# Twelve maxima of the second softmax phase moved into the product stage, tail maxima in pairs, the first tile's scores and exponentials spread over the phase steps

## The reference

```
query = hidden_states @ Wq ; keyt = enc @ Wk ; valt = enc @ Wv
hs      = _mha(query, keyt, valt)                       # 2048 rows against 150 keys
ca_q1   = einsum('btc,th->bch', ca, Wq_ca)[:, indices]  # indices: 384 rows spread over 2048
ca_hs1  = _mha(ca_q1, residual, residual)               # 384 distinct queries against 2048 rows of x
ca_hs2  = _mha(ca_hs1 @ Wq, ca @ Wk_ca, ca @ Wv_ca)     # against 4 tokens
out     = (hs + ca_hs2) @ Wout + b_out + residual
```

## Time and profile before

| | |
|---|---|
| Median of 3 runs | 1694.64 us (1678.9 to 1694.96) |
| The profiled execution's own time | 1688.81 us |
| Its span | 1687.0 us |
| Granted TensorE clock, mean | 0.957 |
| PE busy | 1591.4 us, 94% |
| DVE busy | 811.0 us, 48% |
| ACT busy | 623.1 us, 37% |
| Chain that ended last | PE 86%, DVE 6%, ACT 4% |

### The profile page before, as it was taken

One profiled execution on the slowest core, in us unless ns is written; L12 is line 12 of the kernel. 1 busy time (PEld: TensorE's weight loads), 2 busy tenths in 40 slices (PEclk: granted clock), 3 DMA queues, 4 the chain that ended last, 5 costly groups with the idle time before them and its releaser, 6 DMA issues.

```text
span 1687.0 us, 24707 instructions
## 1 busy us (share of the span) xinstructions
PE 1591.4 (94%) x10327; PEld 1283.8 (76%) x10327; DVE 811.0 (48%) x1624; ACT 623.1 (37%) x1309; POOL 2.8 (0%) x12
## 2 busy tenths in 40 slices
PE   6699989999999989999999998999999999899999
PEld 5584379899986338999988435999898733898998
DVE  4457453453446724435335654354444672534533
ACT  0144742233242662323324275233233357322422
POOL 0000000000000000000000000000000000000000
PEclk9798999999999889999999799999999978999999
DMA  3461001130153000213025200112103500011101
GB/s 128 159 203 58 1 18 48 52 143 16 40 183 117 32 1 18 90 49 112 24 94 175 86 1 7 51 60 84 67 32 142 173 32 1 18 60 63 71 17 40
DMA packets 46793, 116.66 MB, mean 69 GB/s; under 512 B 3661, under 2 KB 5445, under 8 KB 45147
## 3 DMA queue, kind: packets, MB, share of 16 engines
q1 hardware_dynamic: 36180, 92.38, 15.7%
q10 hardware_dynamic: 10503, 22.71, 3.5%
HBM read 76.70 MB, written 38.37 MB: 68 GB/s over the span
## 4 chain that ended last, share of the span: by engine, by line
PE 86%; DVE 6%; ACT 4%; issue 2%; DMA 1%; ACTq 0%; SPq 0%; DVEq 0%
PE ps_w L465 44%; PE ps_s L465 17%; PE ps_t L465 15%; PE ps_t L475 9%; DVE unit_max L1164 3%; ACT work L1001 2%; DVE ot L1328 1%; ACT ot L1029 1%; PE ps_s L475 1%; DMA work<-in_ctx_dram 1%; ACT work L982 0%; DMA ca_rows<-in_ctx_dram 0%; PE ps_w L475 0%; ACT work L909 0%; DVE neg_max L1211 0%
## 5 line engine op out<-in xcount | busy, mean ns | idle before, releaser
L465 PE MATMUL ps_w<-wo_h,ot 128*128 128x320 f32 x1280 | 327.7, 321 | 1.0 <-DVE ot L1328 1.0
L1164 DVE TENSOR_REDUCE unit_max<-ps_s 128x1 f32<-128x512 f32 x384 | 244.1, 685 | 85.7 <-PE ps_s L465 83.4
L465 PEld LDWEIGHTS ps_w<-wo_h,ot 128*128 128x128 f32 x1280 | 222.1, 188 | 2.0 <-DVE ot L1328 2.0
L465 PE MATMUL ps_w<-wo_l,ot 128*128 128x320 f32 x640 | 197.3, 308 | 0.0
L465 PEld LDWEIGHTS ps_w<-v_all,work 120*128 120x128 f32 x1280 | 178.0, 198 | 9.9 <-issue 9.9
L465 PE MATMUL ps_w<-v_all,work 120*128 120x162 f32 (+1 forms) x1280 | 179.3, 297 | 0.0
L982 ACT ACTIVATE work<-ps_s,neg_max 128x150 f32<-128x150 f32 x512 | 154.9, 394 | 44.8 <-DVE neg_max L1215 44.8
L475 PE MATMUL ps_t<-ident,work 128*120 128x128 f32 (+1 forms) x960 | 140.2, 277 | 8.7 <-ACT work L966 4.5
L465 PE MATMUL ps_w<-work,y_all 128*32 128x384 f32 (+1 forms) x1084 | 140.1, 563 | 2.4 <-ACT work L1001 2.3
L966 ACT ACTIVATE work<-ps_t 120x512 f32<-120x512 f32 (+1 forms) x128 | 62.8, 491 | 211.9 <-PE ps_t L475 211.9
L465 PE MATMUL ps_s<-keys_h,qt_h 128*128 128x300 f32 (+1 forms) x448 | 134.2, 299 | 0.0
(11 more groups left out here) (153 smaller groups left out, 2309.9 us busy)
## 6 DMA issues: line engine op xcount, KB each, us to landing
xc<-in_x_dram SPq DMA_DIRECT2D x32, 1280.0 KB, 6.7
out_dram<-work ACTq DMA_DIRECT2D x64, 320.0 KB, 2.2
xt_all<-work SPq DMA_DIRECT2D x60, 256.0 KB, 2.5
xt_l<-xt_all SPq DMA_DIRECT2D x12, 1280.0 KB, 5.6
y_all<-in_L_xattn_Wk_dram SPq DMA_DIRECT2D x4, 960.0 KB
y_all<-in_L_xattn_Wv_dram SPq DMA_DIRECT2D x4, 960.0 KB
pick<-in_pick_dram SPq DMA_DIRECT2D x16, 194.0 KB
xc<-in_L_xattn_Wq_dram SPq DMA_DIRECT2D x1, 1600.0 KB, 7.2
```

What stands on the lines that cost most here:

```text
L465: return nc.tensor.matmul(out, lhs, rhs, start=start, stop=stop, skip_group_check=True)
L1164: v.tensor_reduce(unit_max[:, n, q:q + 1], bank, AX_X, ALU.max).then_inc(max_free, 1)
```

## The change

- **Order of the units.** A table `UNIT_ORDER` replaces the arithmetic: after the 12 phase-0 units of chunks 0 and 1 come the first 6 phase-1 units of that chunk. So 60 units stand ahead of `place_maxima(0)` and 36 behind it. `unit_max` gets a phase index.
- **Product stage.** `UNIT_STEPS` gives each of the steps 8 to 20 a group of 4 or 3 units (before: 2 or 3). Nine groups per batch have four units. `M_BANKS` stays 3. Steps 18 to 20 have 2 queries each instead of 4.
- **Tail.** 9 queries, `turn_g(3)`, 3 queries, then the 12 remaining units in six pairs with 3 queries behind each.
- **DVE.** The order of the low parts and of the copy to `ca_mat` (`take_ca`) changes with it.
- **Phase 0.** 36 units, 3 in each step until they are used up. `tile_scores(0)` parts 0 and 1 and `turn_ca(1)` stand in steps 12 and 13.
- **Phase 1.** ACT takes tile 0's eight exponentials one by one in steps 1 to 8. `turn_z(0)` stands after step 10.
- **Tile 0.** `gather(0)` moves to tile 1, ahead of `turn_weights(1)`; on DVE the shares stand behind tile 0's `turned_weights`, and `picked(0)` behind `maximum(2)`.

```diff
+        if s == 1:
+            order.append(("gather", 0))
         order += [("p", s, part) for part in range(3)]
-        if s == 0:
-            order.append(("gather", 0))
...
-UNITS_BEFORE_SPLIT, UNITS_BEFORE_LOW = 7, 10
-Q0_FILL = [0] * 8 + [4, 4, 4, 3, 0, 4, 4, 4, 3, 0, 4, 4, 4]
-Q0_TAIL, Q0_CHAIN = 2, 3
+UNITS_EARLY = 6
+def unit_order():
+    early, late = [], []
+    for q in range(CHUNKS):
+        units = [(ct, r) for ct in range(CT) for r in range(GROUPS)]
+        early += [(0, q, ct, r) for ct, r in units]
+        n = UNITS_EARLY if q + 2 < CHUNKS else 0
+        early += [(1, q, ct, r) for ct, r in units[:n]]
+        late += [(1, q, ct, r) for ct, r in units[n:]]
+    return early + late, len(early)
+UNIT_ORDER, PHASE0_UNITS = unit_order()
+UNIT_STEPS = {8: 4, 9: 4, 10: 4, 11: 3, 12: 3, 13: 4, 14: 4, 15: 4, 16: 3, 17: 3, 18: 4, 19: 4, 20: 4}
+UNITS_AHEAD_AT = (11, 16, 20)
+UNITS_BEFORE_SPLIT, UNITS_BEFORE_LOW = 12, 15
+Q0_FILL = [0] * 8 + [4, 4, 4, 3, 0, 4, 4, 4, 3, 0, 2, 2, 2]
+Q0_SPLIT, Q0_TURNED, Q0_PAIR, Q0_CHAIN = 9, 3, 3, 3
+UNITS_STEP = 3
...
-                    if phase and u % M_BANKS == T_BANK and u < UNITS + M_BANKS:
+                    if u % M_BANKS == T_BANK and PHASE0_UNITS <= u < PHASE0_UNITS + M_BANKS:
...
-                    max_units(*UNITS_AHEAD[m])
+                    units = UNIT_STEPS.get(m, 0)
+                    if m in UNITS_AHEAD_AT:
+                        max_units(first, units)
...
-                    max_units(*UNITS_AFTER[m])
+                    if m not in UNITS_AHEAD_AT:
+                        max_units(first, units)
+                    first += units
...
-                for u in range(TAIL, UNITS):
-                    n = Q0_MM * 3 - done if u == TAIL else Q0_TAIL if KT * Q0_MM - done > 3 * Q0_CHAIN else 0
-                    queries0(done, n)
-                    done += n
-                    max_unit(u)
-                    if u == TAIL + 2:
-                        turn_g(CHUNKS - 1)
-                queries0(done, Q0_CHAIN)
+                queries0(done, Q0_SPLIT)
+                turn_g(CHUNKS - 1)
+                done += Q0_SPLIT
+                queries0(done, Q0_TURNED)
+                done += Q0_TURNED
+                for u in range(first, PHASE0_UNITS, 2):
+                    max_units(u, 2)
+                    queries0(done, Q0_PAIR)
+                    done += Q0_PAIR
...
+                queries0(done, Q0_CHAIN)
                 turn_ca(0)
                 queries0(done + Q0_CHAIN, KT * Q0_MM)
-                max_units(UNITS, 2)
+                max_units(PHASE0_UNITS, 2)
                 scores(0, 0)
+                first = PHASE0_UNITS + 2
                 for st in range(NST):
                     if st + 1 < NST:
                         scores(0, st + 1)
-                    max_units(UNITS + 2 + 3 * st, 3 if st + 1 < NST else 1)
+                    units = min(UNITS_STEP, PHASES * UNITS - first)
+                    max_units(first, units)
+                    first += units
                     weigh(0, st)
-                tile_scores(0, (0,))
-                turn_ca(1)
-                tile_scores(0, (1,))
+                    if st == 12:
+                        tile_scores(0, (0,))
+                    if st == 13:
+                        turn_ca(1)
+                        tile_scores(0, (1,))
                 scores(1, 0)
                 tile_scores(0, (2,))
...
-                    if st == 7:
+                    if st == 10:
                         turn_z(0)
...
+                    if s == 1:
+                        pe.wait_ge(ot_low, tile0 + 1)
+                        gather(0)
                     turn_weights(s, (0, 1))
                     if s:
                         project(s - 1, 0)
                     turn_weights(s, (2,))
-                    if s == 0:
-                        gather(0)
...
-                        if a and st == 3:
-                            weights(0)
+                        if a and 1 <= st <= HEADS:
+                            if st == 1:
+                                act.wait_ge(nmax_ready, tile0 + 1)
+                            last = weight(0, st - 1)
+                            if st == HEADS:
+                                last.then_inc(p_ready, 1)
...
-                    unit_maxima(first, UNITS_BEFORE_SPLIT)
+                    chunk = per_chunk + (UNITS_EARLY if i < CHUNKS - 1 else 0)
+                    unit_maxima(first, UNITS_BEFORE_SPLIT)
                     split_g(i)
...
-                maximum(1)
-                dve.wait_ge(e2_ready, b + 1)
-                shares.done(v.tensor_reduce(s2_max[:, :], by_head(p2), AX_X, ALU.add))
...
-                pick_window(0)
                 for s in range(SLOTS):
...
-                    if s and s + 1 < SLOTS:
+                    if s + 1 < SLOTS:
                         maximum(s + 1)
+                    if s == 1:
+                        picked(0)
...
                     turned_weights(s)
+                    if s == 0:
+                        dve.wait_ge(e2_ready, b + 1)
+                        shares.done(v.tensor_reduce(s2_max[:, :], by_head(p2), AX_X, ALU.add))
...
+                        pick_window(0)
```

More of the change, by code:

```diff
@@ L127 @@
 E_BUFS = 2
-def unit_steps():
-    ahead, after, u = [(0, 0)] * (GX + 1), [(0, 0)] * (GX + 1), 0
-    for q in range(CHUNKS - 1):
-        for step, (n, table) in enumerate(((2, after), (3, after), (2, after), (3, ahead), (2, after))):
-            m = KT * q + KT + 3 + step
-            if m <= GX:
-                table[m] = (u, n)
-                u += n
-    return ahead, after, u
-UNITS_AHEAD, UNITS_AFTER, TAIL = unit_steps()
-UNITS_BEFORE_SPLIT, UNITS_BEFORE_LOW = 7, 10
-Q0_FILL = [0] * 8 + [4, 4, 4, 3, 0, 4, 4, 4, 3, 0, 4, 4, 4]
-Q0_TAIL, Q0_CHAIN = 2, 3
+UNITS_EARLY = 6
[15 more added lines that the diff above has]
+UNITS_STEP = 3
 def turned_pieces():
@@ L237, in cross_attention @@
         gst = sb("gst", [P, ST, HEADS, RUNG])
-        unit_max = sb("unit_max", [P, CT * GROUPS, CHUNKS])
+        unit_max = sb("unit_max", [P, PHASES, CT * GROUPS, CHUNKS])
         row_max = sb("row_max", [P, CT, GROUPS])
@@ L381, in unit @@
         def unit(u):
-            phase, v = divmod(u, UNITS)
-            q, v = divmod(v, CT * GROUPS)
-            ct, r = divmod(v, GROUPS)
-            return phase, q, ct, r, ps_s[:, u % M_BANKS, :]
+            return (*UNIT_ORDER[u], ps_s[:, u % M_BANKS, :])
         @block.sync
@@ L624, in queries0 @@
                             last.then_inc(q0_full, 1)
-                done = 0
+                done, first = 0, 0
                 for m in range(GX + 1):
@@ L1175, in place_maxima, with take_ca @@
                     v.scalar_tensor_tensor(low.bitcast(F32R), row_max[:, :, :], -1.0, high, ALU.mult, ALU.subtract).then_inc(cst_max, 1)
+                def take_ca(a):
                     dve.wait_ge(ca_full, b * PHASES + a + 1)
@@ L1188, in _ @@
                 split_g(0)
+                first = 0
                 for i in range(1, CHUNKS):
-                    first = (i - 1) * per_chunk
+                    chunk = per_chunk + (UNITS_EARLY if i < CHUNKS - 1 else 0)
                     unit_maxima(first, UNITS_BEFORE_SPLIT)
                     split_g(i)
-                    unit_maxima(first + UNITS_BEFORE_SPLIT, UNITS_BEFORE_LOW - UNITS_BEFORE_SPLIT)
-                    q0_lows(i - 1)
-                    unit_maxima(first + UNITS_BEFORE_LOW, per_chunk - UNITS_BEFORE_LOW)
+                    if i < CHUNKS - 1:
+                        unit_maxima(first + UNITS_BEFORE_SPLIT, UNITS_BEFORE_LOW - UNITS_BEFORE_SPLIT)
+                        q0_lows(i - 1)
+                        unit_maxima(first + UNITS_BEFORE_LOW, chunk - UNITS_BEFORE_LOW)
+                    first += chunk
                 splits.close()
-                unit_maxima(UNITS - per_chunk, UNITS_BEFORE_SPLIT)
+                q0_lows(2)
+                unit_maxima(first, per_chunk)
+                place_maxima(0)
                 q0_lows(3)
-                unit_maxima(UNITS - per_chunk + UNITS_BEFORE_SPLIT, per_chunk - UNITS_BEFORE_SPLIT)
-                place_maxima(0)
+                take_ca(0)
                 q0_lows(4)
-                unit_maxima(UNITS, UNITS)
+                unit_maxima(PHASE0_UNITS, PHASES * UNITS - PHASE0_UNITS)
                 place_maxima(1)
+                take_ca(1)
                 maxima.close()
@@ L1294, in add_rows @@
                                     ALU.add).then_inc((ya_ready, y_ready)[half], 1)
-                maximum(1)
-                dve.wait_ge(e2_ready, b + 1)
-                shares.done(v.tensor_reduce(s2_max[:, :], by_head(p2), AX_X, ALU.add))
-                shares.done(v.reciprocal(s2_max[:, :], s2_max[:, :]))
-                shares.done(v.tensor_tensor(by_head(p2), by_head(p2), spread_t, ALU.mult))
-                for r in range(3):
-                    last = v.tensor_copy(p2_rep[:, :, r, :], p2[:, :, :])
```

(17 more changed lines are left out.)

25 lines of the change are left out of this document (14 added, 11 removed).

## The result

The changed kernel takes **1727.46 us** (median of 4 runs, 1720.06 to 1737.61) against 1690.72 for the kernel before beside it (4 runs, 1678.9 to 1694.96): a ratio of 1.0233, 95% interval 1.0156 to 1.031. The forecast was 1671 us, range 1650 to 1702. It was wrong in sign, and the time lies outside the range. The kernel became slower; whether by more or by less than 2% the interval leaves open. The profiled execution took 1727.67 us (before 1688.81) with a mean granted clock of 0.943 (before 0.957).

The account below looks back on a forecast made before the run. PE was taken to bound the product stage and later tiles, DVE phase 0. Per batch +11.0 - 7.6 - 2.3 - 3.2 - 3.3 = -5.4 us, -21.6 for four, +4 for the clock: 1688.81 to 1671 us, range 1650 to 1702.

Parts of the forecast that it names:

- +1.29 us for each group of four: Product stage: the fourth unit waits for one of three banks, delaying PE 1.29 us per group; +11.0 us a batch.
- I charge one drop of the clock there in the four batches, +4: Product stage, steps 18 to 20: one clock fall in all four batches together, +4 us.
- rival B: Clock falls in the product stage, making the kernel slower: three falls a batch 1715 us, two 1701; chance 18%.
- The prediction's own sign of being wrong: Product stage: wrong if it grows under 8 or over 14 us, or if 0.50 shows between its steps.
- Given back in tile 1: ... about 2.0: Tile 1: `gather(0)` costs PE 0.9 us, and PE waits about 2.0 behind `maximum(2)` and `picked(0)`.
- The tile 0 half: Tile 0: its copy goes first on DVE and `values` runs at full clock, -6.3 us.
- Tail, -7.6: Tail: six pairs at 1.32 us replace singles, 15.1 us against 23.1; -7.6 for the mean batch.
- Phase 0, -2.3: Phase 0: 12 units fewer and less ACT idleness before phase 1, -2.3 us a batch (0 to -4).
- the three terms: Phase 0: last four steps faster -1.3, ACT's idleness shrinks -2.7, PE work moved into steps 12 and 13 +2.1.
- Phase 1, -3.2: Phase 1: exponentials spread over steps instead of done in one go, -3.2 us a batch (-1 to -4.5).

## Why the prediction was wrong, step by step

- **Product stage, "+1.29 us for each group of four": right.** Over three groups of batch 1 the offset to the kernel before grew to 1.27, 2.55 and 3.82 us. In batch 1 the stage grew by 12.1 us (forecast 11.0), with 2 us at 0.50 at its end, and the waits are for `unit_max`, 0.77 us where 0.86 was forecast. (In two groups that follow close on another, PE waits only 0.17 us, but the three units before are spread over 1.11.)
- **"I charge one drop of the clock there in the four batches, +4": failed, the mis-sized term.** In three batches of four the stage spent 17 us more at 0.50 than in batch 1, and that cost some 7 to 8 us a batch beyond the waits (63.5 and 64.5 against 56.7). In sum 22 us came on top of the forecast's 48. This is rival B's mechanism with a longer fall and a higher price than one fall had in its rows: I had priced stretches of 6 to 9 us and none of 17. The trace of before held one of 20 us, in batch 2, across tail and phase 0; it is the row below (columns as in the earlier trace rows). The prediction's own sign of being wrong, 0.50 between the stage's steps, came. The groups of three had no such stretch in four batches, and both ways of placing the nine fourth units had some; so the falls come with the fourth units. The two also differ in the number of units in the stage (39 and 48), which was not tested apart. The Trainium skill ("TensorE: Matmul & The Clock Gate", "A second HAM failure mode: psum-queue depth-cycling") tells of micro-idling between groups as what makes the clock go to and fro. The trace after fits it; the fourth unit behind the queries shows that the clock also falls with PE busy 3.30 of 3.40 us.

```profile
952.40:972.70 20.30, 18.54 (x95) 7.23 (x93) 12.71 (x24) 9.67 (x13) 0.00 (x0) 0.50 0.18 65
```

- **Tile 1, "Given back in tile 1: ... about 2.0": failed, the missing term: the reload of `pick` stands at nothing in the sum.** `gather(0)` 0.9 and PE's wait 1.78 are there as written. What I did not follow is SP's queue past which `gather(0)` moved: `load_pick(1)` waits for `gather(0)`, so the move delays the reload, and `gather(1)` waits for it in the same tile. Of the 7.7 us by which tile 1 is longer than without the reload in its way (21.7 against 14.0 in batch 0), the wait is 2.95; the two stretches at 0.50, 10.2 us of each tile 1, are the rest. The two buffers take 6.5 us a batch out of tile 1, the cut reload 6.9. Forecast for tiles 0 and 1 together: -13.2; measured: +18.3. The tile 0 half was right (-23.9 against -25.2).
- **Tail, -7.6: mis-sized, -6.1 a batch.** The pairs go at 1.32 us as written (559.47 to 560.79). The stage starts at 0.50, because the product stage ends so: its first ten queries take 0.43 us each instead of 0.233 (553.70 to 557.96), 1.9 us in all. That cost was not in the sum.
- **Phase 0, -2.3: right in size, in part by luck** (-2.35 a batch). In batches with the same 6.8 us at 0.50 the stage took 36.64 us before and 35.2 after, so the rearranged work is worth 1.4, not the 1.9 that the three terms give; the rest came from less time at 0.50 (27 us instead of 42 in the four batches), for which 0.4 had been written. **Phase 1, -3.2: right in cause, a little more was won** (-3.95): the stage runs wholly at full clock, as the kernel before with this part alone shows.
- **The sum.** Errors of +21.9 (product stage), +5.9 (tail), -0.2 (phase 0), -3.0 (phase 1) and +31.5 (tiles) make 56.1 of the 56.7 us between the forecast and the profiled execution (1727.67 less 1671).
- **Chances.** B had 18% and was bounded at 1715; no rival named the `pick` reload. With the 31.5 us of the tiles added, the forecast would have been 1702.5 us: slower than before.

**What stays open** is what exactly brings the clock down in the product stage. The same steps of the changed kernel, batch 1 without a fall and batch 2 right before one, have the same work in them:

```profile
933.70:937.10 3.40, 3.16 (x22) 2.06 (x20) 3.17 (x6) 1.39 (x3) 0.00 (x0) 1.00 0.37 140
524.10:527.50 3.40, 3.21 (x22) 2.11 (x20) 3.13 (x6) 1.43 (x3) 0.00 (x0) 1.00 0.35 134
```

The same code of this stage had 17 us or more at 0.50 in one batch of four (reload in 96 rows and 1), two (two buffers), three (the changed kernel) and four (tile part undone). Each count is from one execution, and the ten executions with the reload in 96 rows and 1 are 23 us apart; so the counts may differ as much between executions as between versions, which was not measured. Whether the idle time, the lone 12-row units, the groups held up at a bank or several of these bring the clock down was not separated. So the cost of such a stage can be given as a chance only: 56.7 us without a fall, 63.5 to 68.3 with one or more.

## What to carry to other kernels

When an instruction moves, look for everything that waits for it on every queue, the refill of its input buffer above all: with a single buffer, a later reader means a later reload. Put extra small matmuls only where their banks are free already: here each one beyond the banks cost 1.27 us, and the series of nine came with half clock that cost 7 to 12 us more in some batches and nothing in others. Before pricing a fall of the clock, look at its length in every batch of the trace. Try the parts of a change alone: here two of them gained 1.3 and 2.0% and were hidden behind two that lost more.

## What the runs showed of the hardware that was not expected

- **One DMA of 97 rows went through one engine of 16.** Its stretch has a DMA share of 0.06 (1/16 is 0.0625) at 20 GB/s, and 194 KB took nearly 10 us. As 96 rows and 1 row the load had a share of 0.27 over 2.0 us, at 99 GB/s, and was over. The profile's DMA view counts 97 packets of 2 KB in both, and beside them 1 packet of under 512 bytes with the single DMA and 17 with the two, as if each engine that takes part sent one (16 and 1). The Trainium skill ("DMA: Bandwidth & Descriptors", "Why a DMA increments its semaphore by 16 and not by 1") says that a copy is spread over the largest number of engines, up to 16, that divides its slowest dimension. By that rule 97 rows give one engine and 96 give sixteen; the two traces agree.
- **The clock fell while PE had almost no idle time**: 3.30 of 3.40 us busy, with one group of three spread over 1.11 us for want of a bank, then 20.5 us at 0.50 in each of three batches. Before that I had taken idleness as the condition.
- **A stretch at 0.50 can last 17 to 20.5 us in a stage in which PE is the limit**, and then costs 7 to 9 us (63.5 against 56.7 in the changed kernel; 61.2 against 52.5 with the fourth unit behind the queries). In the kernel before no stage of a batch held more than 14.7 us of it, and no product stage any.
